# Context attention of a perceiver layer: keys kept in natural order, queries made in the even batch, all sums on GpSimd

## What is computed

```python
q_hk = (hidden_q @ Wq.T).reshape(Bv, Sv, H, K)            # 32 x 64 rows, 16 heads
q_big = _apply_rope(jnp.einsum('bshk,hkq->bshq', q_hk, w_kc_q), sin_q, cos_q)
kv_r = _apply_rope(kv_c, sin_k, cos_k)                    # kv_c: 32 x 1601 x 64
q_r = jnp.einsum('bshq,hqr->bhsr', q_big, W_qr)
k_r = jnp.einsum('bld,hdr->bhlr', kv_r, W_kr)
scores = jnp.einsum('bhsr,bhlr->bhsl', q_r, k_r)
attn = jax.nn.softmax(scores, axis=-1)
ctx_c = jnp.einsum('bhsl,bld->bhsd', attn, kv_r)
...
x = x + ctx @ Wo.T
```

## Time and profile before

| | us |
|---|---|
| median of 3 runs | 3501.43 (3490.02 to 3506.24) |
| the profiled execution | 3504.15 |
| its span, first to last instruction | 3501.6 |
| busy: PE, DVE, ACT, POOL | 2942.5, 2084.2, 1277.2, 900.8 |
| context attention, first scores to last | 762.7 to 2625.7 |
| one pair of batches in it | 119.5 |

### The profile page before, as it was taken

One profiled execution on the slowest core, in us unless ns is written; L12 is line 12 of the kernel. 1 busy time (PEld: TensorE's weight loads), 2 busy tenths in 40 slices (PEclk: granted clock), 3 DMA queues, 4 the chain that ended last, 5 costly groups with the idle time before them and its releaser, 6 DMA issues. The chain is left out here.

```text
span 3501.6 us, 51568 instructions
## 1 busy us (share of the span) xinstructions
PE 2942.5 (84%) x17592; PEld 1773.8 (51%) x17592; DVE 2084.2 (60%) x3249; ACT 1277.2 (36%) x2482; POOL 900.8 (26%) x784
## 2 busy tenths in 40 slices
PE   6767734579988988898898889888996889999999
PEld 3544412445544544454455445444543457777776
DVE  3445567357686777677776877686775643333332
ACT  3433312123344343434334433444343333333332
POOL 0001000134354444344434544453440000000000
PEclk9888856679999999999999999999999899999999
DMA  1000030000000000000000000000003000000000
GB/s 39 0 17 0 0 117 0 22 19 10 19 9 19 9 19 9 19 9 19 9 11 17 19 9 9 19 9 19 10 0 145 0 0 0 0 0 0 0 0 25
DMA packets 15045, 57.83 MB, mean 17 GB/s; under 512 B 2512, under 2 KB 7248, under 8 KB 13584
## 3 DMA queue, kind: packets, MB, share of 16 engines
q1 hardware_dynamic: 13392, 53.57, 5.5%
q10 hardware_dynamic: 1600, 3.56, 0.3%
HBM read 55.03 MB, written 2.10 MB: 16 GB/s over the span
## 5 line engine op out<-in xcount | busy, mean ns | idle before, releaser
L917 ACT ACTIVATE cx_prob<-cx_st 128x512 f32<-128x512 f32 (+1 forms) x832 | 477.4, 596 | 742.8 <-PE cx_st L774 680.7
L645 POOL TENSOR_TENSOR cx_acc<-cx_acc,cx_prob 128x512 f32<-128x512 f32 (+1 forms) x352 | 493.8, 1403 | 751.5 <-ACT cx_prob L917 747.4
L1023 DVE TENSOR_REDUCE cx_mhalf<-cx_mx 128x1 f32<-128x804 f32 x512 | 491.2, 983 | 86.5 <-PE cx_mx L747 83.7
L785 PE MATMUL cx_av<-cx_prob,cx_kv 128*64 128x512 f32 (+1 forms) x1664 | 462.2, 635 | 0.0
L773 PE MATMUL cx_st<-cx_q,cx_k 128*128 128x512 f32 (+1 forms) x832 | 372.5, 448 | 84.5 <-ACT cx_prob L917 60.5
L1506 PE MATMUL moe_gu<-moe_wgu,moe_xnT 128*128 128x352 f32 x1280 | 399.0, 463 | 0.0
L1044 DVE TENSOR_TENSOR cx_acc<-cx_acc,cx_prob 128x512 f32<-128x512 f32 (+1 forms) x352 | 371.3, 1055 | 21.7 <-ACT cx_prob L917 19.9
L747 PE MATMUL cx_mx<-cx_k,cx_q 128*128 128x402 f32 x1024 | 309.3, 388 | 53.2 <-DVE cx_mhalf L1023 47.3
L1641 DVE SCALAR_TENSOR_TENSOR moe_hid<-moe_silu,moe_coef,moe_gu 128x176 f32<-128x176 f32 x320 | 127.1, 397 | 351.6 <-ACT moe_silu L1569 349.4
L774 PE MATMUL cx_st<-cx_q,cx_k 128*128 128x512 f32 (+1 forms) x832 | 332.8, 400 | 0.0
L747 PEld LDWEIGHTS cx_mx<-cx_k,cx_q 128*128 128x128 f32 x1024 | 173.4, 195 | 264.0 <-DVE cx_mhalf L1023 216.8
(11 more groups left out here) (214 smaller groups left out, 3945.0 us busy)
## 6 DMA issues: line engine op xcount, KB each, us to landing
cx_ctx<-in_cx_ctxT SPq DMA_DIRECT2D x32, 402.0 KB, 4.3
cx_ctxr<-in_cx_ctxrT SPq DMA_DIRECT2D x32, 402.0 KB, 5.5
moe_wgu<-in_moe_wgu SPq DMA_DIRECT2D x5, 1408.0 KB, 15.3
moe_wd<-in_moe_wd SPq DMA_DIRECT2D x4, 896.0 KB, 25.0
x_all<-in_x SPq DMA_DIRECT2D x1, 2048.0 KB, 5.3
cx_wq<-in_cx_wq SPq DMA_DIRECT2D x1, 2048.0 KB, 12.0
cx_woT<-in_cx_woT SPq DMA_DIRECT2D x1, 2048.0 KB, 29.5
out_x<-x_all SPq DMA_DIRECT2D x1, 2048.0 KB, 7.5
```

Of the source, the lines that this page charges most:

```text
L645: pool.tensor_tensor(acc[0][rows, :], sofar, prob[slot(kt)][rows, 0, :], ALU.add)\
L785: last = pe.matmul(av[DCX * p:DCX * p + DCX, :], kv[e][0:nk(kt), kt, :], prob[slot(kt)][0:nk(kt), p, :], start=(kt == 0), stop=(kt == NKT ...
L917: act.activation(prob[slot(kt)][rows, p, :], st[p][rows, :], ACT.Exp).then_inc(s_exp, 1)
L1023: dve.tensor_reduce(mhalf[:, i // 2, i % 2:i % 2 + 1], mx[i % 2][:, :, 0:KQ], AX.XY, ALU.max)\
```

## The change

Keys are now fetched in natural order (128 keys on the partitions, 13 tiles of 64 numbers, 128x832 in all). POOL does all four elementwise steps on them: two multiplications and the sum (L655, L657, L664), and, after ACT has made the coarse part (`keep_kh`, L908), the remainder (`keep_kl`, L668). Values are a plain copy (`keep_kv`, L915). PE transposes coarse part and remainder together, 13 transposes of 128x128 in four rounds of up to four (`turn_keys`, L728), each round kept by ACT (`keep_turned`, L924) in a new buffer `kp`. `max_scores` reads `kp`; for the scores, two DMAs per batch copy `kp` to `k1` and half of it to `k2` (`move`, L628 and L629 of the new file). Keys are turned two batches ahead and fetched three ahead.

The sums of exponents become one POOL instruction of 128x1024 per pass (`add`, L685), none on DVE, and the ring has four buffers. The queries move to the even batch, passes 7 to 11; ACT keeps them in passes 0 and 1 of the odd batch. The pieces stand in passes 1 to 6 of the even batch and 3 to 9 of the odd one. Both maximum rows are made in pass 11, in the `mx` banks, and `negate_max` stands behind pass 9. The reciprocals are written over `misc`.

```diff
-    RING = 3
+    RING = 4
-    acc = [sb(f"cx_acc{e}", [P, QW]) for e in range(2)]
+    acc = sb("cx_acc", [P, 2, QW])
...
-    OUT_AT = 4
-    TURN_AT = 6
-    ROWS_AT = NKT - 3
-    SUM_AT = (8, 9, 11, 12)
+    OUT_AT = 5
+    SUM_AT = 4
+    KH_AT = 6
+    KL_AT = 7
+    TURN_AT = 7
+    QUERIES_AT = 7
+    NORM_AT = 10
+    NEGATE_AT = 9
+    ROWS_AT = 11
...
-        start, end = 3 * (5 if e else 3), 3 * ROWS_AT
+        start, end = (9, 3 * NEGATE_AT + 3) if e else (4, 3 * QUERIES_AT)
...
+            def move(n, e):
+                sp.wait_ge(s_kp, KROUNDS * (n + 1))
+                if not isinstance(n, int) or n >= 2:
+                    sp.wait_ge(s_st, (n - 1) * 2 * NKT)
+                sp.dma_start(k1[e][:, :].bitcast(F32), kp[e][:, 0:SKP].bitcast(F32)).then_inc(s_kd[e], 16)
+                sp.dma_start(k2[e][0:DCX, :].bitcast(F32), kp[e][0:DCX, 0:SKP].bitcast(F32)).then_inc(s_kd[e], 16)
...
+            def batch(n, t, e, more, next, far):
+                if next:
+                    move(n + 1, 1 - e)
+                if far:
+                    sp.wait_ge(s_kr, n + 3)
+                    fetch(n + 3)
...
             def add(n, kt):
-                pool.wait_ge(s_exp, n * 2 * NKT + 2 * kt + 1)
+                pool.wait_ge(s_exp, n * 2 * NKT + 2 * kt + 2)
...
+                sofar = prob[0][rows, :, :] if kt == 1 else acc[rows, :, :]
+                pool.tensor_tensor(acc[rows, :, :], sofar, prob[slot(kt)][rows, :, :], ALU.add).then_inc(s_acc, 1)
...
                 for kt in range(1, NKT):
                     add(n, kt)
+                    if kt == NORM_AT and far and e == 1:
+                        root(t + 2)
+                    if kt in (NORM_AT - 1, NORM_AT + 1) and far:
+                        rotate(n + 3, kt // NORM_AT)
+                    if kt == SUM_AT and more:
+                        sum_keys(n + 2)
+                    if kt == KL_AT and more:
+                        keep_kl(n + 2)
...
+            def turn_keys(n, r):
+                if r == 0:
+                    pe.wait_ge(s_kl, n + 1)
+                else:
+                    pe.wait_ge(s_kp, KROUNDS * n + r)
+                for kt in range(4 * r, min(4 * r + 4, NKT)):
+                    last = pe.transpose(misc[:, kt % 4 * P:(kt % 4 + 1) * P], khl[:, kt, :, :], ident[:, :])
...
             def denominators(n):
-                for p in range(2):
-                    pe.wait_ge(s_acc[p], (n + 1) * NSUM)
+                pe.wait_ge(s_acc, (n + 1) * NSUM)
```

More of the change, by code:

```diff
@@ L746, in max_scores @@
                     lo = (2 * b + h) * KQ
-                    last = pe.matmul(mx[b][:, h, 0:KQ], q, k1[e][:, lo:lo + KQ], start=True, stop=True)
+                    last = pe.matmul(mx[b][:, h, 0:KQ], q, kp[e][:, lo:lo + KQ], start=True, stop=True)
                 last.then_inc(s_mx, 1)
@@ L815, in before, with batch @@
                     max_scores(0, 0, 0, i)
+                for r in range(KROUNDS):
+                    turn_keys(1, r)
                 max_rows(0, 0)
                 max_rows(0, 1)
-                scores(0, 0, 0, 0)
-                scores(0, 0, 0, 1)
-            def batch(n, t, e, more, next):
+                scores(0, 0, 0, 0, 0)
+                scores(0, 0, 0, 0, 1)
+            def batch(n, t, e, more, next, far):
                 for kt in range(NKT):
-                    if kt == 0 and more and e == 1:
-                        turn_x(t + 1)
                     for third in range(3):
@@ L840, in batch @@
                         out(t - 1)
-                    if kt in (TURN_AT, TURN_AT + 1) and next:
+                    if 0 <= kt - TURN_AT < KROUNDS and more:
                         if kt == TURN_AT and not is_first(n):
@@ L938, in before, with batch @@
                     keep_queries(0, g)
+                keep_kh(1)
+                for r in range(KROUNDS):
+                    keep_turned(1, 0, 1, r)
                 keep_rows(0, 0, 0)
                 keep_rows(0, 0, 1)
-            def batch(n, t, e, more, next):
+            def batch(n, t, e, more, next, far):
                 for kt in range(NKT):
@@ L1094, in batch @@
                         odd_queries(t)
-                    if kt == 1 and next:
-                        keep_kl(n + 1, 1 - e)
+                    if kt in (1, 2) and more and e == 1:
+                        split(t + 1, kt - 1)
                     if kt in (HEADS_AT, HEADS_AT + 1) and not is_first(n):
```

286 lines of the change are left out of this document (133 added, 153 removed).

## The result

The change makes the kernel faster: 3397.02 us (median of 4 runs, 3391.70 to 3399.73) against 3502.89 for the kernel before, a ratio of 0.9706 with a 95% interval of 0.9684 to 0.9727. That is 106 us, where 42 were forecast. The profiled execution has a span of 3394.7 us, against 3501.6 before.

A forecast was written before the change was run, and what follows sets the result against it. PE was taken to bound the attention stage, idling 13.3 us per pair; new waits of 10.3 saved 3.0 per pair, 46.5 over 15.5 pairs, less 4 at the start: 42 us saved, forecast 3459, range 3388 to 3522.

The forecast's parts named there:

- PE's work: PE's busy time per pair of batches: transposes cost about the same as before, so 0, bounds 0 and +0.5 us.
- Waits gone: PE's waits for DVE, per pair: maximum rows' 3.1 us and heads' 1.3 go, kept rows' 1.5 shrinks.
- The pieces against DVE: PE waiting for DVE's maxima: 3.4 us in the even batch, 0.7 in the odd, together 4.1, bounds 1.5 and 5.5.
- ACT: PE waiting for exponents behind ACT's copies, at batch starts and around pass 11: 4.5 us per pair, bounds 3 and 6.
- POOL: POOL's sums at 2.35 us: no bound; new wait of 1.3 at `keep_kl`, none at `denominators` by 0.2 us.
- rival C: POOL comes last: longer POOL instructions make `denominators` wait 2.7 us and `keep_kl` add 1.0; 3516 us, chance 0.17.
- SP: The `move` copies of keys, 1206 KB within SBUF per batch: price taken as 0.
- Rival D: Slower: `move` holds up the next fetch, POOL and the denominators; decides from a 26 us copy; 3574 us, chance 0.14.
- Start: Start of the stage: eight rounds of PE and ACT replace two, +4 us once, the wider last sum's +1 within that.
- The sum: Per pair: new waits 10.3 us against old 13.3, so 3.0 less, for 15.5 pairs, less 4 at the start.
- Rival B: Waits mostly vanish: half of the pieces' and ACT's terms stand, PE idle under 7 us per pair; 3392 us, chance 0.17.
- The forecast's own bounds: Bounds on pieces (1.5 to 5.5), ACT (3 to 6) and PE's 0.5, said to give about 3410 to 3505 us.

The follow-up runs named there:

- e_kv_later: Kernel after with one number changed: ACT's copy to `kv` stands in pass 2 instead of pass 1; 3360.9 us.
- e_before_pool_sums: Kernel before with only the sums of exponents changed: both go to POOL as one 128x1024 add per pass, ring still three; 3518.0 us.
- e_rows: Kernel before with only the maximum rows changed: written to `mx`, both in pass 11; 3444.4 us.
- e_queries_odd: Kernel after with queries, their copies, rotations, splits and the pieces back where they stood before; 3335.6 us.

## Why the prediction was wrong

The direction, the range (3388 to 3522) and most places were right. The forecast of 3459 lies 62 us above the result. Two terms of its sum were mis-sized, by about as much each: PE's own work, put at 0, fell by 2.4 us a pair, and the new waits, put at 10.3, came to 7.7. By its own steps, per pair:

- **PE's work, taken as 0 with bounds 0 and +0.5: this step failed.** PE's busy time fell by 2.4 us, beyond the bounds. The sum counted instructions and took their durations as fixed. The trace of before already had 15 stretches at half clock in 14 pairs, 13 of them behind the wait of 1.98 that the second group of query copies makes in the odd batch, and I never priced them. One of these waits (PE; the stretch began 1.5 us later and lasted 3.41):

```profile
1327.81 0.50 PE L773 MATMUL cx_st<-cx_q,cx_k 128*128 128x512 f32 x1 [1.98 <-ACT cx_prob L917]
```

e_kv_later shows the coupling: 0.8 us of wait brings 1.0 of busy time with it. Five stretches fewer account for 0.6 of the 2.4. By line (each matmul counted to the start of the next) the 2.4 lie on pieces (0.8), scores (0.8), rows and keys (0.6) and the rest (0.2). A second part is the number of stops, however short: a matmul of the pieces takes 0.45 us right behind a stop and 0.35 otherwise (medians in before). Counting every stop over 0.03 us, PE stops 15.1 times a pair in before, 10.0 in after and 9.9 in e_before_pool_sums, which has 15 stretches as before has and 1.0 us less of busy time, 0.9 of it at the pieces. By that, an estimate, five fewer stops give another 1.0. The last 0.8 are open.
- **Waits gone: right in what, wrong in why.** The waits for `nml`, kept rows and `heads` are gone. The prediction said that a queue of sums stood in front of the negation. Taking that queue away alone made the wait longer, 3.2 to 6.1 a pair. What stood there were the keys' sums and the cast, and the longer POOL sum holds both. The rows' new place alone took 2.3 of the 3.2. Nor has the holding gone from after: in 13 of 28 batches the last step of the negation still takes 2.2 us beside a POOL sum instead of 0.17. It ends before pass 11, where the rows now stand, so PE doesn't wait for it:

```profile
1428.64 2.23 DVE L1070 TENSOR_TENSOR cx_nml<-cx_nmax,cx_nmh 128x8 bf16<-128x8 f32 x1
```

- **The pieces against DVE, 4.1: measured 3.6**, and 0.2 in front of the transposes of `x`. The walk through passes 2 to 4 gave 0.9 + 0.4 + 1.7 + 0.4 in the even batch; the rows show 0.87 and 1.66, so the two small ones were covered. In the odd batch it is 1.05 for 0.7.
- **ACT, 4.5: measured 3.3.** Pass 2 of the odd batch 1.81 for 2.3 and pass 1 0.47 for 0.5; pass 12 0.49 and 0.48 for 0.7 each; the even batch's start nothing for 0.3. The copy to `kv` took 0.89, estimated at 0.86.
- **POOL: the lengths right, 2.34 to 2.40 for 2.35 and 1.96 to 1.97 for 1.94.** The wait for `keep_kl` was 0.35 for 1.3, the denominators 0.38 for 0 with a margin of 0.2. The twelve sums are the race that they were taken for; rival C had put 2.7 there. (PE's five passes in that sum add up to 13.6, not 13.5.)
- **SP: right.** Rival D falls: no move took more than 7.3 us, where it needed 26.
- **Start.** First scores 3.1 us later for 4; but at the end POOL's last sums cost 5.9 us, where I had left 1 for it.
- **The sum.** Waits of 10.3 forecast and 7.7 measured, 2.6 too many, and 2.4 of busy time missing: together 7.9 us a pair and not 3.0. The 14 pairs gave 110.5 us where 15.5 pairs were to give 46.5; the ends cost 3.6 us for 4. Rival B's number, 3392, was nearly met, but not its condition: PE idles 7.7 us a pair, not under 7. Half of the missed gain came from a term that B didn't have either, so B's number was met by luck. The forecast's own bounds, simply added, are wider than the 3410 to 3505 that it names: the low ends (pieces 2.6 and ACT 1.5 less) give 3395, the high ones 3512. So the measured 3397 lies inside them, but by luck too, for PE's work was to grow in them and not to fall.

The parts, as the experiments split them: the rows' place is worth some 60 us (before against e_rows). The keys off DVE and the sums on POOL are worth 109 more together (e_rows to e_queries_odd; the ring, the later `out` and the reciprocals in `misc` are in that number too), though the sums alone cost 16 on before and 36 on e_rows. Moving the queries and pieces to the even batch gives 61 of it back; its pieces are pressed into six passes, around two reciprocals.
